# Loads of x from batch 2 on issued from ScalarE's queue, not from SyncE's

## The chip, the cores and the metric

The kernel runs on one core of a Trainium2 chip. The metric is device time in microseconds (us). The core has five engines that run their own instruction streams in order and meet at semaphores: PE (TensorE), DVE (VectorE), ACT (ScalarE), POOL (GpSimd) and SP (SyncE), which only issues DMAs here. DMAs issued from SP form SP's queue ("SPq" in the profile), those issued from ACT form ACT's ("ACTq").

## What is computed

```python
x = L0_attn_t                                   # (16, 1024, 256) float32
x = x + layernorm(attention(layernorm(x)))      # one head, 256 wide, W_qkv (768, 256) and a bias
x = x + layernorm(ffn(layernorm(x)))            # ffn: down(silu(gate(x)) * up(x)), hidden 768
# attention: softmax(Q K^T / 16) V; the ffn weights are integers times 1/127
```

Every float32 operand is split into a high and a low float16 part, and a product is two or three float16 matmul passes (high by high, high by low, low by high).

## The kernel before, in words

The 16 batches of 1024 rows are worked off in a software pipeline: while PE does the scores of batch b+1, it does the attention output of batch b and then its ffn. Each batch is cut into two halves g (512 rows). The order of the work is written out by hand for every engine; there is no scheduler. Batches 0, 14 and 15 have an order of their own, the ones between run through a loop.

The steps that the change and the prediction touch:

- x is loaded from HBM twice. `load_x(b, g)` (L213) loads a half into `xs`, from which the first layernorm (`x_stats` on DVE, `x_norm` on POOL, `x_hat` on ACT) and the split into `xh` and `xl` (`x_high` on ACT, `x_low` on POOL) are made. It waits until `x_low` of the batch before has read `xs`. `reload(b, g)` (L229) loads the same half into one of four buffers `X`, to which the attention's result is added (`x1_add`, DVE, L664). It waits until the store from that buffer, two batches before, has landed.
- `turn_x`, `turn_p`, `turn_y` (L218, L237, L247) are DMA transposes in SBUF, each for a high and a low part: `xTh`/`xTl`, `PTh`/`PTl` (the softmax numerators), `yTh`/`yTl` (the ffn's input). `store` (L254) writes the result out. All of them are issued by SP, in one hand-written order, with a wait ahead of each. In the period of batch b the loads stand behind `turn_x(b+2, 1)` and ahead of `turn_p(b+1, 7)` and `turn_y(b, 1)`.
- The ffn's input of a half is made in this chain: `x1_norm` (POOL, writes `nb`), `y_hat` (ACT, L458, writes `yn`), `y_high` (ACT, L465, writes `yh`), `y_low` (POOL, L365, writes `yl`), `turn_y` (SP, L251), and then `gate_up` on PE, which needs both transposes.
- `exp` (ACT, L438) and `p_high` (ACT, L445) make a block of softmax numerators; `p_low` (L338) is the low part. `silu` (ACT, L473) and `h_high` (ACT, L480) belong to the ffn. Exp and silu need different function tables, so that ACT loads a table at each change between them (ACT_TABLE_LOAD).
- All matmul passes are issued in one helper, L710, so PE's rows carry that line. PE's `gate_up(b, g, c)` waits for its PSUM bank with a `silu_done` count, as in `gate_up(t, 0, 0, 4, 2, (silu_done, 2), (hmul_done, 2), three)` (L1796).

Of the kernel before, what the change touches and what calls it, by code (L numbers as in the profile page):

```python
# [40 lines left out]
def sandwich(nc, x_d, wqkv_d, b_d, wg_d, wu_d, wd_d, out_d):  # L41
# [8 lines left out]
    with ctx:  # L50
# [162 lines left out]
        def load_x(s, b, g):  # L213
            xl_wait(s, b - 1, g)
            s.engine.dma_start(xs[:, 4 * g:4 * g + 4, :],
                               x_d[b, :, :].rearrange("(p t) d -> p t d", t=NT)[:, 4 * g:4 * g + 4, :]).then_inc(xs_in[g], 16)
# [12 lines left out]
        def reload(s, b, g):  # L229
            k = (2 * b + g) % 4  # L230
            s.wait_ge(stored[k], 32 * (b // 2))
            if b < 2:
                s.wait_ge(ffn_turned[b], 32)
            s.engine.dma_start(X[k][:, :, :], x_d[b, :, :].rearrange("(p t) d -> p t d", t=NT)[:, 4 * g:4 * g + 4, :]
                               ).then_inc(X_in[k], 16)
# [608 lines left out]
        def _(engine):  # L844
# [23 lines left out]
            turn_p(s, 0, 3, 1)  # L868
            turn_x(s, 1, 1, 0)
            turn_x(s, 1, 1, 1)  # L870
            load_x(s, 2, 0)
            load_x(s, 2, 1)
            turn_p(s, 0, 4, 0)
            turn_p(s, 0, 4, 1)
            turn_p(s, 0, 5, 0)
# [10 lines left out]
            turn_p(s, 1, 0, 1)  # L886
            turn_ffn(s, 2, 0)
            turn_ffn(s, 2, 1)
            reload(s, 0, 0)
            reload(s, 0, 1)  # L890
            turn_p(s, 1, 1, 0)
            turn_p(s, 1, 1, 1)
            turn_p(s, 1, 2, 0)
# [8 lines left out]
            turn_y(s, 0, 0, 1)  # L902
            turn_x(s, 2, 1, 0)
            turn_x(s, 2, 1, 1)
            load_x(s, 3, 0)
            load_x(s, 3, 1)
            turn_p(s, 1, 5, 0)
            turn_p(s, 1, 5, 1)
            turn_p(s, 1, 6, 0)
# [3 lines left out]
            turn_p(s, 1, 7, 0)  # L913
            turn_p(s, 1, 7, 1)
            for b in range(1, 13):
                reload(s, b, 0)
                reload(s, b, 1)
                turn_p(s, b + 1, 0, 0)
                turn_p(s, b + 1, 0, 1)
                store(s, b - 1, 0, 0)  # L920
                store(s, b - 1, 0, 1)
                turn_p(s, b + 1, 1, 0)
                turn_p(s, b + 1, 1, 1)
                turn_p(s, b + 1, 2, 0)
                turn_p(s, b + 1, 2, 1)
                turn_p(s, b + 1, 3, 0)
                turn_p(s, b + 1, 3, 1)
                turn_p(s, b + 1, 4, 0)
                turn_p(s, b + 1, 4, 1)
                turn_y(s, b, 0, 0)  # L930
                turn_y(s, b, 0, 1)
                turn_x(s, b + 2, 0, 0)
                turn_x(s, b + 2, 0, 1)
                turn_p(s, b + 1, 5, 0)
                turn_p(s, b + 1, 5, 1)
                turn_p(s, b + 1, 6, 0)
                turn_p(s, b + 1, 6, 1)
                turn_x(s, b + 2, 1, 0)
                turn_x(s, b + 2, 1, 1)
                load_x(s, b + 3, 0)  # L940
                load_x(s, b + 3, 1)
                turn_p(s, b + 1, 7, 0)
                turn_p(s, b + 1, 7, 1)
                turn_y(s, b, 1, 0)
                turn_y(s, b, 1, 1)
                store(s, b - 1, 1, 0)
                store(s, b - 1, 1, 1)
            reload(s, 13, 0)
            reload(s, 13, 1)
            turn_p(s, 14, 0, 0)  # L950
            turn_p(s, 14, 0, 1)
            store(s, 12, 0, 0)
# [22 lines left out]
            turn_y(s, 13, 1, 1)  # L975
            store(s, 12, 1, 0)
            store(s, 12, 1, 1)
            reload(s, 14, 0)
            reload(s, 14, 1)
            store(s, 13, 0, 0)  # L980
            turn_p(s, 15, 0, 0)
            turn_p(s, 15, 0, 1)
# [18 lines left out]
            turn_p(s, 15, 7, 0)  # L1001
            turn_p(s, 15, 7, 1)
            store(s, 13, 1, 1)
            reload(s, 15, 0)
            reload(s, 15, 1)
            store(s, 14, 0, 0)
            store(s, 14, 0, 1)
            turn_y(s, 15, 0, 0)
# [167 lines left out]
        def _(engine):  # L1176
# [23 lines left out]
            exp(a, 0, 5, 6)  # L1200
            z_high(a, 1, 0, 2)
            p_high(a, 0, 5)
            exp(a, 0, 6, 0)
            p_high(a, 0, 6)
            ffn_high(a, 0)
# [9 lines left out]
            exp(a, 1, 1, 2)  # L1215
            p_high(a, 1, 1)
            x_hat(a, 2, 0)
            exp(a, 1, 2, 0)
            p_high(a, 1, 2)
            exp(a, 1, 3, 2)  # L1220
# [13 lines left out]
            p_high(a, 1, 6)  # L1234
            exp(a, 1, 7, 2)
            p_high(a, 1, 7)
            silu(a, 0, 0, 0, 6)
            y_hat(a, 0, 1, 0)
            y_hat(a, 0, 1, 1)
# [25 lines left out]
            x_hat(a, 3, 0)  # L1265
            h_high(a, 0, 1, 5)
            x_hat(a, 3, 1)
            exp(a, 2, 0, 0)
            p_high(a, 2, 0)
            o_high(a, 1, 0, 1)  # L1270
# [4 lines left out]
            for b in range(2, 14):  # L1275
                p_high(a, b, 1)
                exp(a, b, 2, 0)
                p_high(a, b, 2)
                exp(a, b, 3, 2)
                p_high(a, b, 3)  # L1280
                o_high(a, b - 1, 1, 1)
                exp(a, b, 4, 0)
                p_high(a, b, 4)
                y_hat(a, b - 1, 0, 0)
                y_hat(a, b - 1, 0, 1)
                y_high(a, b - 1, 0)
                o_high(a, b - 1, 1, 0)
                x_high(a, b + 1, 0)
                exp(a, b, 5, 2)
                p_high(a, b, 5)  # L1290
                x_high(a, b + 1, 1)
                exp(a, b, 6, 0)
                p_high(a, b, 6)
                exp(a, b, 7, 2)
                p_high(a, b, 7)
                silu(a, b - 1, 0, 0, 6)
                z_high(a, b + 1, 0, 0)
                h_high(a, b - 1, 0, 0)
                silu(a, b - 1, 0, 1, 2)
                y_hat(a, b - 1, 1, 0)  # L1300
                y_hat(a, b - 1, 1, 1)
                y_high(a, b - 1, 1)
                h_high(a, b - 1, 0, 1)
                silu(a, b - 1, 0, 2, 6)
                h_high(a, b - 1, 0, 2)
                silu(a, b - 1, 0, 3, 0)
                silu(a, b - 1, 0, 4, 2)
                h_high(a, b - 1, 0, 3)
                z_high(a, b + 1, 1, 6)
                h_high(a, b - 1, 0, 4)  # L1310
                silu(a, b - 1, 0, 5, 0)
                silu(a, b - 1, 1, 0, 2)
                h_high(a, b - 1, 0, 5)
                silu(a, b - 1, 1, 1, 6)
                add_bias(a, b - 2, 1, 0)
                h_high(a, b - 1, 1, 0)
                silu(a, b - 1, 1, 2, 0)
                h_high(a, b - 1, 1, 1)
                silu(a, b - 1, 1, 3, 2)
                add_bias(a, b - 2, 1, 1)  # L1320
                h_high(a, b - 1, 1, 2)
                silu(a, b - 1, 1, 4, 6)
                h_high(a, b - 1, 1, 3)
                silu(a, b - 1, 1, 5, 0)
                h_high(a, b - 1, 1, 4)
                h_high(a, b - 1, 1, 5)
                exp(a, b + 1, 0, 0)
                p_high(a, b + 1, 0)
                o_high(a, b, 0, 1)
                add_bias(a, b - 1, 0, 0)  # L1330
                o_high(a, b, 0, 0)
                x_hat(a, b + 2, 0)
                add_bias(a, b - 1, 0, 1)
                exp(a, b + 1, 1, 2)
                x_hat(a, b + 2, 1)
# [48 lines left out]
            silu(a, 13, 1, 5, 0)  # L1384
            h_high(a, 13, 1, 4)
            h_high(a, 13, 1, 5)
            o_high(a, 14, 0, 1)
            o_high(a, 14, 0, 0)
            add_bias(a, 13, 0, 0)
# [42 lines left out]
            h_high(a, 14, 1, 0)  # L1432
            h_high(a, 14, 1, 1)
            silu(a, 14, 1, 2, 0)
            h_high(a, 14, 1, 2)
            o_high(a, 15, 0, 1)
            add_bias(a, 14, 0, 0)
# [581 lines left out]
```

## Time and profile before

| | |
|---|---|
| median of 3 runs | 1376.56 us (1376.06 to 1376.75) |
| profiled execution, its time | 1376.6 us |
| its span in the trace | 1374.7 us |
| PE busy | 1352.9 us, 98% |
| DVE, ACT, POOL busy | 65%, 64%, 60% |
| granted TensorE clock | 0.999 of full speed |
| DMA, queue of SP | 54.4% of the 16 DMA engines' time |

The span runs from the first to the last instruction of the profiled execution; 1.9 us of its time lie around it. PE is the engine that is nearly always busy, so the reader should look for the few places where it is not, and follow from each to what it waited for. Busy shares of the others matter only where they end such a wait.

### The profile page before, as it was taken

Reading aid. Unit: us, or ns where it says so; the run is one execution under the profiler, and the core shown is the slowest. Engines: PE = TensorE matmul, PEld = TensorE weight load, DVE = VectorE, ACT = ScalarE, POOL = GpSimd, SP = SyncE. Lnnn points to the kernel's source line nnn. Section 1 sums busy time; section 2 is a strip of 40 time slices with the busy share of each in tenths; the row PEclk is TensorE's granted clock in tenths of the full one; section 3 lists DMA queues with packets and bytes.
Section 4 is the critical chain, followed back from the end, with each engine's and each line's share of the span. In section 5 each row is a group of like instructions: output and inputs, shape, how many; then the busy total and the mean of one; then the engine's idle time right before and its main releaser. Section 6 shows DMA issues by size and latency. Waiting matters only on the chain.

```text
span 1374.7 us, 22429 instructions
## 1 busy us (share of the span) xinstructions
PE 1352.9 (98%) x7437; PEld 728.8 (53%) x7437; DVE 897.3 (65%) x2160; ACT 877.5 (64%) x1373; POOL 825.2 (60%) x1002
## 2 busy tenths in 40 slices
PE   8999999999999999999999999999999999999997
PEld 4444555554555555555554555545555555555554
DVE  6786666666757667666766657667566666656555
ACT  4757475766756667575675767567566775756644
POOL 2768375573837658476484756748376583745545
PEclk9999999999999999999999999999999999999999
DMA  7996382654727466382753836447383663716411
GB/s 199 188 185 149 68 163 78 116 130 84 147 85 135 104 112 143 77 163 68 137 132 70 161 77 123 123 95 144 78 151 88 123 133 80 141 55 114 94 40 55
DMA packets 437176, 158.29 MB, mean 115 GB/s; under 512 B 418113, under 2 KB 420417, under 8 KB 437058
## 3 DMA queue, kind: packets, MB, share of 16 engines
q1 hardware_dynamic: 436272, 156.03, 54.4%
q8 instruction: 61, 1.00, 0.3%
q10 hardware_dynamic: 786, 0.79, 0.2%
q14 instruction: 57, 0.47, 0.1%
HBM read 36.70 MB, written 16.78 MB: 39 GB/s over the span
## 4 chain that ended last, share of the span: by engine, by line
PE 91%; DVE 3%; SPq 2%; DMA 2%; issue 1%; POOL 1%; ACT 0%; ACTq 0%; POOLq 0%
PE S L710 90%; DMA yTl<-yl 1%; SPq L245 1%; PE S L729 1%; DVE mxs L613 1%; DVE S L642 0%; SPq L226 0%; DVE st L651 0%; POOL rs L293 0%; SPq L251 0%; DMA xTl<-xl 0%; POOL Pl L338 0%; DVE xl L320 0%; POOL yl L365 0%; DVE X L664 0%
## 5 line engine op out<-in xcount | busy, mean ns | idle before, releaser
L438 ACT ACTIVATE P<-S,nmx,sc 128x1024 f32<-128x1024 f32 x128 | 153.6, 1200 | 283.1 <-DVE nmx L617 283.1
L613 DVE TENSOR_REDUCE mxs<-S 128x1 f32<-128x1024 f32 x128 | 156.1, 1220 | 124.7 <-PE S L710 124.4
L679 DVE SCALAR_TENSOR_TENSOR hf<-S,sc,hf 128x512 f32<-128x512 f32 x192 | 141.9, 746 | 140.6 <-ACT hf L473 134.4
L338 POOL TENSOR_TENSOR Pl<-P,Ph 128x1024 f16<-128x1024 f32 x96 | 205.9, 2145 | 33.9 <-issue 26.4
L710 PE MATMUL S<-xTh,zTh 128*128 128x512 f16 x512 | 194.1, 379 | 4.2 <-ACT P L438 2.2
L710 PE MATMUL S<-PTh,xl 128*128 128x512 f16 x512 | 194.0, 379 | 0.0
L710 PE MATMUL S<-xTl,zTh 128*128 128x512 f16 x512 | 194.0, 379 | 0.0
L710 PE MATMUL S<-xTh,zTl 128*128 128x512 f16 x512 | 194.0, 379 | 0.0
L710 PE MATMUL S<-PTl,xh 128*128 128x512 f16 x512 | 194.0, 379 | 0.0
L710 PE MATMUL S<-PTh,xh 128*128 128x512 f16 x512 | 194.0, 379 | 0.0
L289 POOL TENSOR_SCALAR rs<-mv,sc 128x2 f32<-128x2 f32 (+1 forms) x96 | 35.2, 367 | 231.5 <-DVE mv L655 191.8
L710 PE MATMUL S<-Wh,hTh 128*128 128x256 f16 x768 | 170.4, 273 | 1.9 <-DVE X L703 1.7
L374 POOL TENSOR_TENSOR hTl<-hf,hTh 128x512 f16<-128x512 f32 x128 | 146.2, 1157 | 41.0 <-ACT hTh L480 36.7
L710 PE MATMUL S<-Wh,hTl 128*128 128x256 f16 x768 | 170.4, 273 | 0.0
L473 ACT ACTIVATE hf<-S,sc 128x512 f32<-128x512 f32 x192 | 130.7, 682 | 53.1 <-POOL hTl L374 35.4
L293 POOL TENSOR_TENSOR rs<-rs,mhalf 128x4 f32<-128x4 f32 (+1 forms) x160 | 145.0, 906 | 13.3
L710 PE MATMUL S<-yTh,Gh 128*128 128x512 f16 x384 | 145.6, 379 | 4.0 <-DMA yTl<-yl 3.9
L710 PE MATMUL S<-yTl,Gh 128*128 128x512 f16 x384 | 145.5, 379 | 0.0
L710 PE MATMUL S<-yTh,Uh 128*128 128x512 f16 x384 | 145.5, 379 | 0.0
L710 PE MATMUL S<-yTl,Uh 128*128 128x512 f16 x384 | 145.5, 379 | 0.0
L480 ACT ACTIVATE hTh<-hf 128x512 f16<-128x512 f32 x192 | 119.8, 624 | 33.8 <-DVE hf L679 33.8
L445 ACT ACTIVATE Ph<-P 128x1024 f16<-128x1024 f32 x128 | 135.1, 1055 | 5.6 <-DMA PTl<-Pl 2.0
(115 smaller groups left out, 2476.1 us busy)
## 6 DMA issues: line engine op xcount, KB each, us to landing
xs<-in_L_attn_t SPq DMA_DIRECT2D x32, 512.0 KB, 5.3
X<-in_L_attn_t SPq DMA_DIRECT2D x32, 512.0 KB, 4.4
out_x<-X SPq DMA_DIRECT2D x64, 256.0 KB, 2.9
PTh<-Ph SPq DMA_TRANSPOSE x128, 3.2
PTl<-Pl SPq DMA_TRANSPOSE x128, 3.2
hTh<-in_L_attn_W_qkv ACTq DMA_DIRECT2D x1, 768.0 KB, 7.2
hTl<-in_L_ffn_w_gate SPq DMA_DIRECT2D x1, 768.0 KB, 7.4
hTh<-in_L_ffn_w_up SPq DMA_DIRECT2D x1, 768.0 KB, 9.1
```

Of the source, the lines that this page charges most:

```text
L245: s.engine.dma_start_transpose(dst[:, :, c * 128:(c + 1) * 128], src[:, m % 3, :]).then_inc(p_turned[m % 3], 16)
L289: p.engine.tensor_scalar(rs, var, scalar1=eps, scalar2=mul, op0=ALU.add, **({} if mul is None else {"op1": ALU.mult})).then_inc(g_step, 1)
L293: return p.engine.tensor_tensor(out=rs, in0=rs, in1=mhalf[:, 0:rs.shape[1]], op=ALU.pow)
L338: p.engine.tensor_tensor(out=Pl[:, m % 3, :], in0=P[:, m % 2, :], in1=Ph[:, m % 3, :], op=ALU.subtract).then_inc(pl_vector if i in PL_ON_V ...
L374: p.engine.tensor_tensor(out=hTl[g][:, c, :], in0=hf[:, n % 3, :], in1=hTh[g][:, c, :], op=ALU.subtract).then_inc(hl_vector if c in HL_ON_ ...
L438: a.engine.activation(P[:, m % 2, :], ps[:, bank:bank + 2, :].rearrange("p a n -> p (a n)"), ACT.Exp, bias=nmx[:, c:c + 1], scale=sS, accu ...
L445: a.engine.activation(Ph[:, m % 3, :], P[:, m % 2, :], ACT.Copy).then_inc(ph_done, 1)
L473: a.engine.activation(hf[:, n % 3, :], ps[:, bank, :], ACT.Silu, scale=sc2[:, 3:4]).then_inc(silu_done, 1)
L480: a.engine.activation(hTh[g][:, c, :], hf[:, n % 3, :], ACT.Copy).then_inc(hh_done, 1)
L613: v.engine.tensor_reduce(mxs[:, c:c + 1], ps[:, bank:bank + 2, :].rearrange("p a n -> p (a n)"), axis=AX.X, op=ALU.max, negate=True).then_ ...
L679: v.engine.scalar_tensor_tensor(out=hf[:, n % 3, :], in0=ps[:, bank + 1, :], scalar=sc2[:, 4:5], in1=hf[:, n % 3, :], op0=ALU.mult, op1=AL ...
L710: done = t.engine.matmul(out, s, m, start=(start and i == 0), stop=(stop and i == len(terms) - 1))
```

## The change

The pairs of `load_x` from batch 2 on and all pairs of `reload` leave SP's list and are put into ACT's list, between activations. Functions and waits are unchanged, only the engine that waits and issues differs, and the place in the order. `load_x` of batches 0 and 1, all transposes and all stores stay on SP.

```diff
@@ SP's list
             turn_x(s, 1, 1, 1)
-            load_x(s, 2, 0)
-            load_x(s, 2, 1)
             turn_p(s, 0, 4, 0)
...
-            reload(s, 0, 0)
-            reload(s, 0, 1)
...
-            load_x(s, 3, 0)
-            load_x(s, 3, 1)
...
             for b in range(1, 13):
-                reload(s, b, 0)
-                reload(s, b, 1)
                 turn_p(s, b + 1, 0, 0)
...
                 turn_x(s, b + 2, 1, 1)
-                load_x(s, b + 3, 0)
-                load_x(s, b + 3, 1)
                 turn_p(s, b + 1, 7, 0)
...
-            reload(s, 13, 0), (s, 13, 1), (s, 14, 0), (s, 14, 1), (s, 15, 0), (s, 15, 1)
@@ ACT's list
             p_high(a, 0, 5)
+            load_x(a, 2, 0)
+            load_x(a, 2, 1)
             exp(a, 0, 6, 0)
...
             x_hat(a, 2, 0)
+            reload(a, 0, 0)
+            reload(a, 0, 1)
             exp(a, 1, 2, 0)
...
             p_high(a, 1, 7)
+            load_x(a, 3, 0)
+            load_x(a, 3, 1)
             silu(a, 0, 0, 0, 6)
...
             x_hat(a, 3, 1)
+            reload(a, 1, 0)
+            reload(a, 1, 1)
             exp(a, 2, 0, 0)
...
@@ ACT's loop, for b in range(2, 14)
                 silu(a, b - 1, 0, 1, 2)
+                load_x(a, b + 2, 0)
+                load_x(a, b + 2, 1)
                 y_hat(a, b - 1, 1, 0)
...
                 h_high(a, b - 1, 1, 5)
+                reload(a, b, 0)
+                reload(a, b, 1)
                 exp(a, b + 1, 0, 0)
...
             h_high(a, 13, 1, 5)
+            reload(a, 14, 0)
+            reload(a, 14, 1)
             o_high(a, 14, 0, 1)
...
             silu(a, 14, 1, 2, 0)
+            reload(a, 15, 0)
+            reload(a, 15, 1)
             h_high(a, 14, 1, 2)
```

## Rows read from the trace of the kernel before

**Rows 1.** The page: span and busy time of each engine.

```profile
span 1374.7 us, 22429 instructions
...
PE 1352.9 (98%) x7437; PEld 728.8 (53%) x7437; DVE 897.3 (65%) x2160; ACT 877.5 (64%) x1373; POOL 825.2 (60%) x1002
```

**Rows 2.** Busy time by stretch: stretch, length, busy us of each engine, PE clock, DMA share.

```profile
318.00:401.00 83.00, 83.00 (x457) 44.61 (x456) 54.77 (x132) 54.43 (x87) 51.34 (x62) 1.00 0.54 115
```

**Rows 3.** Waits of PE, whole span: waiter, releaser, total us, times, longest.

```profile
PE S L710 <- DMA yTl<-yl: 3.9, 5, 1.8
```

**Rows 4.** Timeline of PE: start us, us, instruction, [idle before, releaser].

```profile
122.92 0.39 PE L710 MATMUL S<-yTh,Gh 128*128 128x512 f16 x1 [0.20 <-DMA yTl<-yl]
...
705.35 0.39 PE L710 MATMUL S<-yTh,Gh 128*128 128x512 f16 x1 [0.58 <-DMA yTl<-yl]
...
955.11 0.39 PE L710 MATMUL S<-yTh,Gh 128*128 128x512 f16 x1 [0.40 <-DMA yTl<-yl]
...
1267.78 0.39 PE L710 MATMUL S<-yTh,Gh 128*128 128x512 f16 x1 [1.01 <-DMA yTl<-yl]
```

**Rows 5.** Timeline of SP's queue near three of these waits; durations are issue times.

```profile
119.47 1.34 SPq L251 DMA_TRANSPOSE yTl<-yl  x1
...
693.15 1.06 SPq L215 DMA_DIRECT2D xs<-in_L_attn_t  x2
694.25 1.42 SPq L245 DMA_TRANSPOSE PTh<-Ph  x1
695.72 4.98 SPq L245 DMA_TRANSPOSE PTl<-Pl  x1
...
702.10 1.32 SPq L251 DMA_TRANSPOSE yTl<-yl  x1
...
951.87 1.31 SPq L251 DMA_TRANSPOSE yTl<-yl  x1
```

**Rows 6.** Timeline of POOL near the same three waits.

```profile
115.32 2.13 POOL L365 TENSOR_TENSOR yl<-yn,yh 128x1024 f16<-128x1024 f32 x1 [0.71 <-ACT yh L465]
...
689.03 2.12 POOL L320 TENSOR_TENSOR xl<-xs,xh 128x1024 f16<-128x1024 f32 x1
...
698.51 2.13 POOL L365 TENSOR_TENSOR yl<-yn,yh 128x1024 f16<-128x1024 f32 x1 [0.51 <-ACT yh L465]
...
948.62 2.14 POOL L365 TENSOR_TENSOR yl<-yn,yh 128x1024 f16<-128x1024 f32 x1 [0.51 <-ACT yh L465]
```

**Rows 7.** Timeline of ACT at the start: a DMA that ACT issues.

```profile
0.72 0.53 ACTq L395 DMA_DIRECT2D ft<-in_L_attn_b_qkv  x1
```

**Rows 8.** Timeline of ACT at the two places in the loop.

```profile
384.26 0.63 ACT L480 ACTIVATE hTh<-hf 128x512 f16<-128x512 f32 x1 [0.37 <-DVE hf L679]
...
394.61 1.21 ACT L438 ACTIVATE P<-S,nmx,sc 128x1024 f32<-128x1024 f32 x1 [8.41 <-DVE nmx L617]
...
692.19 0.70 ACT L473 ACTIVATE hf<-S,sc 128x512 f32<-128x512 f32 x1
695.27 2.08 ACT L458 ACTIVATE yn<-X,nb,rs 128x256 f32<-128x256 f32 x4 [2.38 <-POOL nb L298]
```

**Rows 9.** A pair of reloads on SP, and reloads on the page (last: us to landing).

```profile
381.60 2.46 SPq L234 DMA_DIRECT2D X<-in_L_attn_t  x2
...
X<-in_L_attn_t SPq DMA_DIRECT2D x32, 512.0 KB, 4.4
```

**Rows 10.** Timeline of DVE: first use of a reloaded X.

```profile
415.24 0.87 DVE L664 SCALAR_TENSOR_TENSOR X<-S,rs,X 128x256 f32<-128x256 f32 x2
```

**Rows 11.** Timeline of ACT and of PE near the loads of batch 3.

```profile
108.13 1.06 ACT L445 ACTIVATE Ph<-P 128x1024 f16<-128x1024 f32 x1
...
115.66 1.25 ACT L473 ACTIVATE hf<-S,sc 128x512 f32<-128x512 f32 x2
...
116.52 0.38 PE L710 MATMUL S<-yTh,Gh 128*128 128x512 f16 x1
```

**Rows 12.** Busy time of a stretch of 1 us while loads land, columns as in rows 2.

```profile
365.00:366.00 1.00, 1.00 (x6) 0.48 (x5) 0.00 (x0) 1.00 (x2) 0.39 (x2) 1.00 0.98 389
```

More of the change, by code:

```diff
@@ L947, in _ @@
                 store(s, b - 1, 1, 1)
-            reload(s, 13, 0)
-            reload(s, 13, 1)
             turn_p(s, 14, 0, 0)
@@ L977, in _ @@
             store(s, 12, 1, 1)
-            reload(s, 14, 0)
-            reload(s, 14, 1)
             store(s, 13, 0, 0)
@@ L1003, in _ @@
             store(s, 13, 1, 1)
-            reload(s, 15, 0)
-            reload(s, 15, 1)
             store(s, 14, 0, 0)
```

## The prediction

> **What bounds the kernel now.** I read the first page, then PE's busy time stretch by stretch, then PE's waits, then each place where PE stood idle, and from there back through SP's queue, POOL and ACT. PE is busy for 98% of the span [rows 1], and the chain is nearly all PE's. From 152 us to 1231 us the kernel repeats a period of 83 us (13 of them), in which PE is busy from end to end; row 2 is one of them [rows 2]. So what another engine or a queue does there shows only where PE is made to wait. The list of PE's waits has one cause that transposes and loads share: the landing of yTl, 3.9 us in five places [rows 3]. Two of these are in the repeated part, 0.58 us at 705.35 and 0.40 us at 955.11; one of 0.20 us is at 122.92, one of 1.01 us at 1267.78 [rows 4]. The fifth, the longest of rows 3 (1.8 us), is at 107 us.
>
> How the two in the repeated part come about: SP issues the two loads of x in 1.06 us, then the transpose to PTh, and then holds for 4.98 us on the transpose to PTl, so that yTl is issued at 702.10 [rows 5]. POOL had yl ready at 698.51 + 2.13 = 700.64 [rows 6]. SP was thus 1.46 us late. At the other place yl was ready at 948.62 + 2.14 = 950.76 and yTl issued at 951.87, 1.11 us late [rows 5, 6]. PE waited 0.58 and 0.40 us, less than SP was late in both. In the other periods SP shows the same hold after the loads, but PE does not wait.
>
> **The change, part by part.**
> Off SP: 28 loads of xs (batches 2 to 15) and 32 reloads of X, in pairs of about 1.06 us. Every transpose on SP behind a pair of loads may start up to 1.06 us sooner. If the long hold of PTl is that SP's own queue is full of the two loads, it goes too; then yTl is issued as soon as yl is there, and the 0.58 and 0.40 us close: **-0.98 us**. The other 10 periods have no PE wait to give back. At 1267.78 no load stands near on SP (the reload of batch 14 is 50 us earlier), so those 1.01 us stay; and at 107 us yTl was issued ahead of the loads of batch 3. The lower bound of this term is nothing (the hold stays), the upper all that rows 3 has, 3.9 us.
>
> Onto ACT, what one pair costs: a DMA that ACT issued in this trace took 0.53 us [rows 7], two of them 1.06, as SP's pair did [rows 5]. I take 1.06. Below that it can be nothing, if ACT's issue runs beside the activation before it; above I use 2.46, SP's pair of reloads with a wait in it [rows 9].
>
> *Loads in the loop, 12 times*, stand between a silu and y_hat. The silu starts at 692.19 and takes 0.70; y_hat starts at 695.27 and stood idle for 2.38 us for POOL's nb [rows 8]. 1.06 fits in 2.38, and even 2.46 leaves only 0.08. The wait that comes along (x_low of the batch before) is on POOL ahead of a p_low and the x1_norm that y_hat waits for: xl ended at 689.03 + 2.12 = 691.15 [rows 6], before the silu began. So the wait is met. Cost 0. Without that cover, 1.06 us a period would go into the chain y_hat, y_high, y_low, yTl, against 704.77 - (700.64 + 0.05 + 3.20) = 0.88 us that yTl could then be late (704.77 is when PE could have begun; 3.20 is what yTl took to land).
>
> *Reloads in the loop* stand ahead of exp(b+1, 0), after the last h_high at 384.26 + 0.63. That exp begins at 394.61 after 8.41 us idle [rows 8], with the table load of 1.28 us ahead of this idle time. Their wait is for the stores of two batches before; SP met the same wait by 381.60 + 2.46 = 384.06 [rows 9], before ACT is there. Cost 0, with over 7 us to spare. X then lands some 4.4 us after issue [rows 9], near 390.5; its first use is at 415.24 [rows 10]. Cost 0. The pairs outside the loop, read off ACT's timeline in the same way, stand in or just ahead of idle time of ACT that is longer than a pair, but for the reload of batch 15, which lacks 0.1 us, and for the next one.
>
> *Loads of batch 3* are the one place without cover: behind p_high(1, 7), with the table load and silu(0, 0, 0) right behind it. ACT is then in arrears up to the silu pair at 115.66, whose first ends near 116.30; gate_up(0, 0, 4) needs it and starts at 116.52 [rows 11]: 0.22 us of slack. A delay d of ACT becomes d - 0.22 on PE. The ends are d = 0 and 1.06 (0 and 0.84 us); activations start before the last one has ended and the issue may lie under the 1.06 us of p_high, so I take the middle, 0.53: **+0.31 us**. The later yTl is not hurt: POOL made yl ready at 115.32 + 2.13 = 117.45 [rows 6], which becomes 117.98, and SP issued yTl only at 119.47 [rows 5], behind the loads and the same hold. There are 1.49 us to use, so the 0.20 us at 122.92 close: **-0.20 us**.
>
> *DMA engines.* The bytes are the same and the loads start within 1 us of before. In the stretch with loads the engines are near full (0.98 busy at 389 GB/s in the microsecond at 365 us, where loads land) [rows 12], so the work is there on any queue; what may change is who stands behind whom.
>
> **Sum:** -0.98 + 0.31 - 0.20 = -0.87 us. The profiled execution took 1376.6 us (span 1374.7), the median of the runs 1376.56, so the sum is applied as it stands: 1375.7.
>
> **Rivals.**
> *The hold stays.* The hold of PTl is the DMA engines at work on the loads, not SP's queue. Then the transposes issued beside the loads share the engines with them, PTl is held as long as before, and yTl gains nothing. For it: rows 12. Against it: yTl comes last and the work ahead of it, two loads and two transposes, must anyway be over before yl is ready. Time: 0 for the two gaps, and 0 to 0.84 us at batch 3: 1376.6 to 1377.4, say 1377.0. The Trainium skill, "DMA: Bandwidth & Descriptors", section "Issuing engines are not separate DMA queues", says that DMAs from different engines run on the same 16 DMA engines and interleave, and that only the sequencer's issue time is saved. By that rule alone this rival holds; its sum would be 1377.0 against my 1375.7. The trace of before can't decide, as all loads in it beside transposes come from SP.
>
> *ACT is held at its issue (the other side).* If ACT's pair of loads meets the hold that PTl met, the in-order engine stops before y_hat. Place: the 12 periods. It decides from 2.38 + 0.88 = 3.26 us per pair; at 3.5 us the loss, 12 x 0.24, passes 0.2%. With a first load of 0.53 and a second held as PTl was, 4.98 us, a pair takes 5.5: 12 x 2.25 = 27 us, and 5.3 at batch 3, so up to 1409. Against it: SP's own two loads, right behind transposes, took 1.06 us and were never held; the one held is the second transpose after them [rows 5], and ACT's queue carries nothing else.
>
> *More than two gaps go.* If transposes land sooner without loads ahead of them, all 3.9 us could close: 1372.7. Against it: at 107 us and 1267.78 no load stands ahead.
>
> **How the numbers follow.** Forecast 0.50 (1375.7, own range 1375.2 to 1376.4); hold stays 0.30 (1377.0); ACT held 0.10 (over 1379.3); more gaps 0.04; the rest, an unforeseen shift of 1 to 2 us at the ends, 0.06. The runs spread by 0.7 us, and about 0.2% (2.75 us) is what can be told from no change. The range runs from 1374.4, with part of the other gaps closed, to 1378.8, which is a pair of 2.46 us on ACT (2.24 at batch 3) and no gap closed. Faster 0.04, same 0.85, slower 0.11.
>
> **What would show it.** PTl after the loads takes about 1.3 us at issue and not 3 to 5; yTl is issued within 0.1 us of yl's end; the waits of PE for yTl are near 2.7 us, not 3.9; ACT's idle time before y_hat is near 1.3 and not 2.4 us; a gap of 0.3 us or so opens in PE near 115 to 117 us; ACT's pair takes about 1.06. The prediction is wrong if ACT's idle time before y_hat is gone and PE waits for yTl in every period.

## The result, and the profile after

The changed kernel takes 1424.84 us (median of 6 runs), the kernel before 1376.53 in the same series: 1.036 times as long, 95% interval 1.034 to 1.038. That is 48 us slower, where 1375.7 was forecast and 1378.8 was the upper end.

The page after, and PE's waits (waiter, releaser, total us, times, longest):

```profile
span 1425.1 us, 22429 instructions
...
PE 1369.6 (96%) x7437; PEld 731.6 (51%) x7437; DVE 897.8 (63%) x2160; ACT 881.4 (62%) x1373; POOL 822.0 (58%) x1002
...
q1 hardware_dynamic: 427632, 124.57, 48.1%
q10 hardware_dynamic: 9426, 32.25, 8.6%
```

```profile
PE S L710 <- DMA xTl<-xl: 35.0, 11, 5.4
PE S L710 <- DMA yTl<-yl: 2.8, 4, 1.0
```

Against [rows 3] the wait for yTl has shrunk from 3.9 to 2.8 us, and a new one is there: PE waits for xTl, the low part of the transposed x of batch b+2, 35.0 us in 11 places. Nine of them are in the loop; of the other two one is at the start, as before (1.4 us against 1.3), and one of 0.91 us at 59.84. The span is 50.4 us longer. PE's idle time grew from 1374.7 - 1352.9 = 21.8 to 1425.1 - 1369.6 = 55.5 us, that is by 33.7. The other 16.7 us are PE's own: the same 7437 matmuls are busy for longer.

One of these places, on SP's queue, on ACT and on PE (start us, us, instruction, [idle before, releaser]):

```profile
193.90 1.34 SPq L226 DMA_TRANSPOSE xTh<-xh  x1
195.28 1.34 SPq L226 DMA_TRANSPOSE xTl<-xl  x1
196.67 3.94 SPq L245 DMA_TRANSPOSE PTh<-Ph  x1
200.66 8.36 SPq L245 DMA_TRANSPOSE PTl<-Pl  x1
209.11 1.33 SPq L251 DMA_TRANSPOSE yTh<-yh  x1
```

```profile
195.14 0.33 ACTq L215 DMA_DIRECT2D xs<-in_L_attn_t  x1
195.20 0.64 ACT L480 ACTIVATE hTh<-hf 128x512 f16<-128x512 f32 x1
195.52 0.48 ACTq L215 DMA_DIRECT2D xs<-in_L_attn_t  x1
195.72 0.69 ACT L473 ACTIVATE hf<-S,sc 128x512 f32<-128x512 f32 x1
198.77 2.08 ACT L458 ACTIVATE yn<-X,nb,rs 128x256 f32<-128x256 f32 x4 [2.36 <-POOL nb L298]
```

```profile
209.41 0.61 PE L710 MATMUL S<-xTh,Ah 128*128 128x512 f16 x1 [5.43 <-DMA xTl<-xl]
209.81 0.63 PE L710 MATMUL S<-xTl,Ah 128*128 128x512 f16 x1
```

The same place on SP's queue in the kernel before:

```profile
193.14 1.35 SPq L226 DMA_TRANSPOSE xTl<-xl  x1
194.53 1.06 SPq L215 DMA_DIRECT2D xs<-in_L_attn_t  x2
195.63 1.68 SPq L245 DMA_TRANSPOSE PTh<-Ph  x1
197.36 3.10 SPq L245 DMA_TRANSPOSE PTl<-Pl  x1
```

The two loads are issued by ACT within 0.4 us, just as SP issues xTl. xTl lands at 209.4, 14.1 us after issue (4.6 before). Of the two loads the first lands 5.5 us after issue and the second, caught in the same stall, 13.7. SP is then held for 3.9 and 8.4 us at the next two transposes, where it took 1.7 and 3.1 before (and 1.4 and 5.0 in the period of [rows 5]). ACT pays nothing: the two DMA instructions run beside activations, and its idle time before y_hat is 2.36 us, as before.

What xTl took to land, whole span, of the kernel before and then of the one after:

```profile
DMA to landing us min/median/max: 3.1/3.3/5.0
```

```profile
DMA to landing us min/median/max: 3.2/4.2/14.1
```

For the second halves in the 12 periods of the loop it is 3.1 to 4.9 us before (the loads are issued 1.4 us behind xTl), and after it is 10.8 to 14.1 in nine and 6.9 to 7.6 in three. PE wanted it 8.7 us after issue here (PE was ready at 203.98) and 7.8 to 8.7 in the 12, so it waits in the nine and not in the three. The nine and the three differ in the moment: in the nine ACT issued the first load 0.1 to 0.4 us ahead of SP's xTl, in the three 0.75 and 0.91 us ahead of it or 0.24 behind it.

The stretch of the wait, in slices of one us (columns as in [rows 2]: the last three are the granted PE clock, the DMA share and GB/s):

```profile
202.00:203.00 1.00, 1.00 (x7) 0.44 (x5) 0.00 (x0) 1.00 (x2) 0.99 (x1) 1.00 1.03 169
...
205.00:206.00 1.00, 0.00 (x0) 0.00 (x0) 1.00 (x2) 0.78 (x2) 1.00 (x2) 1.00 1.72 23
206.00:207.00 1.00, 0.00 (x0) 0.00 (x0) 1.00 (x2) 0.54 (x2) 1.00 (x2) 1.00 0.87 53
207.00:208.00 1.00, 0.00 (x0) 0.00 (x0) 0.90 (x3) 0.12 (x1) 1.00 (x2) 0.67 1.30 71
208.00:209.00 1.00, 0.00 (x0) 0.00 (x0) 0.00 (x0) 0.00 (x0) 0.92 (x2) 0.50 1.23 42
...
213.00:214.00 1.00, 1.00 (x4) 0.30 (x2) 0.72 (x1) 0.00 (x0) 0.00 (x0) 0.50 0.08 16
214.00:215.00 1.00, 1.00 (x6) 0.45 (x5) 0.00 (x0) 0.46 (x1) 0.00 (x0) 0.92 0.00 0
```

Two things are to be seen. The DMA engines count as fully busy while they move 23 to 71 GB/s, where they move 389 in [rows 12] and 210 with transposes alone (share 1.12, at 105 us of the kernel before): they are occupied and hardly move data. (A packet's whole time is counted in the slice in which it starts, so a slice can show a share above 1.) And PE, idle since 203.98, is granted 1.2 GHz instead of 2.4 from 207.3 to 214.1 us: the matmuls after the wait follow each other in 0.43 us instead of 0.22. The clock fell so behind seven of the nine waits in the loop (2.87 to 5.43 us long), not behind the other two (2.19 and 2.82 us), and also near 105 and 1412 us. This is where the 16.7 us of longer PE busy time lie; the mean granted clock fell from 0.999 to 0.987, and 1.2% of 1425 us is 17 us.

### The profile page after: what moved, and what is told of

It reads as the page before. It is cut to its first block, busy times and chain, and to the rows that moved or that the text cites. A ratio compares the mean times of both kernels' runs of the same rounds, so it can differ in the third digit from the quotient of the medians.

```text
span 1425.1 us, 22429 instructions
## 1 busy us (share of the span) xinstructions
PE 1369.6 (96%) x7437; PEld 731.6 (51%) x7437; DVE 897.8 (63%) x2160; ACT 881.4 (62%) x1373; POOL 822.0 (58%) x1002
## 4 chain that ended last, share of the span: by engine, by line
PE 80%; DMA 8%; DVE 4%; SPq 4%; issue 2%; ACT 2%; POOL 1%; ACTq 0%; POOLq 0%
PE S L710 79%; DMA xTl<-xl 7%; SPq L245 2%; SPq L226 1%; DVE mxs L613 1%; DVE S L642 1%; DVE st L651 1%; DMA yTl<-yl 1%; ACT Ph L445 1%; PE S L729 1%; ACT P L438 0%; POOL Pl L338 0%; DVE mv L655 0%; DVE nmx L617 0%; SPq L251 0%
## 5 line engine op out<-in xcount | busy, mean ns | idle before, releaser
L710 PE MATMUL S<-xTh,zTh 128*128 128x512 f16 x512 | 194.7, 380 | 5.1 <-ACT P L438 2.2
L710 PE MATMUL S<-xTh,zTl 128*128 128x512 f16 x512 | 194.7, 380 | 0.0
L710 PE MATMUL S<-xTl,zTh 128*128 128x512 f16 x512 | 194.6, 380 | 0.0
L710 PE MATMUL S<-PTh,xh 128*128 128x512 f16 x512 | 194.1, 379 | 0.1
L710 PE MATMUL S<-PTl,xh 128*128 128x512 f16 x512 | 194.1, 379 | 0.0
L710 PE MATMUL S<-PTh,xl 128*128 128x512 f16 x512 | 194.1, 379 | 0.0
L710 PE MATMUL S<-Wh,hTh 128*128 128x256 f16 x768 | 172.0, 274 | 1.9 <-DVE X L703 1.7
L710 PE MATMUL S<-Wh,hTl 128*128 128x256 f16 x768 | 172.0, 274 | 0.0
L293 POOL TENSOR_TENSOR rs<-rs,mhalf 128x4 f32<-128x4 f32 (+1 forms) x160 | 145.0, 906 | 13.3
L710 PE MATMUL S<-yTh,Gh 128*128 128x512 f16 x384 | 145.8, 380 | 3.8 <-DMA yTl<-yl 2.8
L710 PE MATMUL S<-yTh,Uh 128*128 128x512 f16 x384 | 145.6, 379 | 0.0
L710 PE MATMUL S<-yTl,Gh 128*128 128x512 f16 x384 | 145.6, 379 | 0.0
L710 PE MATMUL S<-yTl,Uh 128*128 128x512 f16 x384 | 145.6, 379 | 0.0
```

What stands on the lines that cost most here:

```text
L293: return p.engine.tensor_tensor(out=rs, in0=rs, in1=mhalf[:, 0:rs.shape[1]], op=ALU.pow)
L710: done = t.engine.matmul(out, s, m, start=(start and i == 0), stop=(stop and i == len(terms) - 1))
```

## The experiments

Times are medians with the ratio to the kernel before run on the same chip. All kernels but the bare stages compute the whole reference. The theories that the texts below name A to G are each stated where they first come up. "The place of the changed kernel" is between silu(b-1, 0, 1) and y_hat(b-1, 1, 0) on ACT. The loads of batches 2 and 3, ahead of the loop, go to ACT in e2_load_only and e10_merged alone, and the reloads in e1_reload_only and e10_merged alone; elsewhere they stay on SP.

### Which of the moved loads it is

**e1_reload_only**: only the reloads move.

```diff
 SP:   (all load_x as before; every reload removed)
 ACT:  reload(a, b, 0); reload(a, b, 1)      # at the places of the changed kernel; no load_x
```

> Only the reloads of X are issued from ACT; the loads of xs stay on SP as before. Theory A (copies from ACT's queue slow the transposes of SP's queue while both are in flight): in the loop the reloads stand where SP issues no transposes, so the time is that of before, 1376.5 us within 1.5 us. Theory B (the loads of xs start ahead of the transposes of x, on whatever queue): also 1376.5. Theory C (any traffic on ACT's queue costs, wherever it stands): a good part of the 48 us, 1395 or more.

Measured: 1376.19 us, ratio 1.000 (0.999 to 1.001). The reloads cost nothing, as forecast, so ACT's queue in itself is not the cause: theory C falls.

**e2_load_only**: only the loads of xs from batch 2 on move.

```diff
 SP:   (every reload as before; load_x from batch 2 on removed)
 ACT:  load_x(a, b + 2, 0); load_x(a, b + 2, 1)      # and batches 2 and 3; no reload
```

> Only the loads of xs are issued from ACT, at the places of the changed kernel; the reloads of X stay on SP. Theory A (copies of ACT's queue beside transposes of SP's queue): all of the loss is here, 1420 to 1430 us, with PE waiting some 35 us for xTl. Theory C (any traffic on ACT's queue): clearly less than the whole loss.

Measured: 1429.32 us, ratio 1.038 (1.034 to 1.042). PE's wait for xTl is 39.5 us in 12 places. The loss lies wholly in the loads of xs.

### Queue, order or moment

**e3_sp_early**: the order of the changed kernel, on one queue.

```diff
+                load_x(s, b + 3, 0)
+                load_x(s, b + 3, 1)
                 turn_x(s, b + 2, 1, 0)
                 turn_x(s, b + 2, 1, 1)
-                load_x(s, b + 3, 0)
-                load_x(s, b + 3, 1)
```

> All loads on SP, but in the loop the pair of loads of xs is moved ahead of the pair of transposes to xTh and xTl, so that it starts as early as in the changed kernel. Theory A (two queues): xTl lands 3 to 7 us after issue and PE waits for it little or not at all, 1376 to 1382 us. Theory B (order alone): xTl lands 10 us or more after issue, PE waits for it in most periods, 1400 us or more.

Measured: 1376.56 us, ratio 1.000 (0.999 to 1.001).

```profile
191.00 1.14 SPq L215 DMA_DIRECT2D xs<-in_L_attn_t  x2
192.19 1.25 SPq L226 DMA_TRANSPOSE xTh<-xh  x1
193.48 3.60 SPq L226 DMA_TRANSPOSE xTl<-xl  x1
```

With 1 MB queued ahead of it, xTl lands in 4.8 to 7.7 us in the loop, and PE waits for it 0.1 us at most. Bytes and order explain 1 to 4 us of landing, not 11. Theory B falls. (SP's pairs are issued 0.6 to 0.8 us apart here and ACT's 0.4 in the changed kernel; the bare stages below bear on that.)

**e4_act_quiet** and **e5_sp_quiet**: the pair is issued where no transposes are in flight, from ACT and from SP.

```diff
 e4, ACT:                h_high(a, b - 1, 1, 2)
+                load_x(a, b + 2, 0)
+                load_x(a, b + 2, 1)
 e5, SP:                 turn_y(s, b, 1, 1)
+                load_x(s, b + 3, 0)
+                load_x(s, b + 3, 1)
                 store(s, b - 1, 1, 0)
```

> In the loop the loads of xs are issued from ACT, but some 15 us later, behind the third h_high of the second half, where SP has no transposes in flight; all else as before. Theory A: no transposes beside them, and no hold of PTl behind them either, so 1375.0 to 1376.5 us. Theory C (ACT's queue costs anywhere): well over 1390 us.

> The same later place with SP as the issuer: in the loop the pair of loads of xs stands behind the transposes to yTh and yTl of the second half. Every theory: PTl is held no longer, yTl is issued as soon as yl is there, the two waits of PE of 0.58 and 0.40 us close: 1375.0 to 1376.5 us. With the run before it, it tells whether the queue matters at all when no transposes are near.

Measured: 1375.08 us, ratio 0.9992 (0.9982 to 1.0001), and 1374.75 us, 0.9992 (0.9983 to 1.0002). Away from transposes the queue makes no difference. Both intervals still include no change. In both, PE's wait for yTl is 2.9 us in 2 places: the gaps of 0.58 and 0.40 us of [rows 4] are gone, and that of 0.20 us too, although the loads of batch 3 stand where they stood. SP's queue in e5_sp_quiet, at the period that had the longest hold in [rows 5]:

```profile
691.97 1.33 SPq L245 DMA_TRANSPOSE PTh<-Ph  x1
693.34 1.49 SPq L245 DMA_TRANSPOSE PTl<-Pl  x1
697.28 1.23 SPq L251 DMA_TRANSPOSE yTh<-yh  x1
699.49 1.24 SPq L251 DMA_TRANSPOSE yTl<-yl  x1
700.77 1.06 SPq L215 DMA_DIRECT2D xs<-in_L_attn_t  x2
```

The hold of PTl (4.98 us) is gone, and yTl is issued 0.03 us after yl is ready (697.33 + 2.13 on POOL).

**e6_one_load**: one of the two loads at the place of the changed kernel, the other on SP as before.

```diff
 SP:                     load_x(s, b + 3, 0)
-                load_x(s, b + 3, 1)
 ACT:                    silu(a, b - 1, 0, 1, 2)
+                load_x(a, b + 2, 1)
                 y_hat(a, b - 1, 1, 0)
```

> In the loop one of the two loads of xs (the second half) is issued from ACT at the place of the changed kernel, the other stays on SP behind the transposes to xT; reloads on SP. Theory A in its plain form (the slowing lasts as long as ACT's queue has copies in flight, here half the bytes): xTl lands 7 to 9 us after issue, PE waits little, 1378 to 1395 us. If one copy is enough to upset the transposes whatever its size: 1410 us or more.

Measured: 1375.15 us, ratio 0.9995 (0.9986 to 1.0005). xTl lands in 5.0 to 6.7 us. Half the bytes from ACT's queue at this place cost nothing at all, less than either reading expected.

**e7_after_xT**: the pair waits until xTh and xTl have landed.

```diff
                 silu(a, b - 1, 0, 1, 2)
+                a.wait_ge(x_turned[1], 32 * (b + 2))
+                load_x(a, b + 2, 0)
+                load_x(a, b + 2, 1)
                 y_hat(a, b - 1, 1, 0)
```

> In the loop the pair of loads of xs is issued from ACT at the place of the changed kernel, but behind a wait until the transposes to xTh and xTl ahead of it have landed; only those to PTh, PTl, yTh and yTl are still in flight beside it. Theory A: xTl lands after 3 to 4 us and PE waits for it no more; the slowing falls on PTl and on yTl, which lands late, so that PE waits there: 1385 to 1415 us. If only the transposes ahead of the loads are slowed: about 1376 to 1380 us, with ACT's short wait.

Measured: 1387.1 us, ratio 1.008 (1.007 to 1.010). The time fell into theory A's range, but not for its reason. xTl lands in 3.3 to 5.0 us in the loop. PE's waits there (152 to 1240 us) show that yTl's grew, from 1.0 to 2.1 us, and that the largest new one is another:

```profile
PE S L710 <- ACT hf L473: 5.8, 7, 1.7
PE S L710 <- DMA yTl<-yl: 2.1, 4, 1.0
```

ACT, which stands and waits for the transposes, is late with what PE needs next. PTl, in flight when the loads are issued, lands in 6.5 to 8.2 us in nine of the 12 periods and in 3.2 to 4.1 in the other three. That is twice and more what it takes in e4_act_quiet (3.1 to 4.5), but little more than in the kernel before (5.7 to 7.2) and far from the 11 to 14 of xTl. yTh and yTl, issued some 4 us and more after the loads, land in 3.0 to 5.8 and 3.0 to 4.4, and SP is held at no transpose of the loop for more than 2.4 us. So the pair of loads does slow what it meets here too, but with PTl and the end of PTh in flight and no transpose right behind them the stall does not come. Whether the number of transposes or the moment matters, this run doesn't tell.

**e8_apart**: both loads on ACT, the second 5.8 us after the first.

```diff
                 silu(a, b - 1, 0, 1, 2)
+                load_x(a, b + 2, 0)
                 y_hat(a, b - 1, 1, 0)
                 y_hat(a, b - 1, 1, 1)
                 y_high(a, b - 1, 1)
+                load_x(a, b + 2, 1)
```

> In the loop both loads of xs are issued from ACT, the first at the place of the changed kernel, the second some 5 us later, behind y_high; all else as before. The plain form of theory A has fallen (in the bare stages two loads from ACT cost no more than two from SP, and with one load from ACT the kernel lost nothing). Theory D (two copies queued on ACT at once beside a full queue of transposes is what upsets them): xTl lands in 5 to 7 us, 1375 to 1378 us. Theory E (bytes from ACT's queue within the stretch of transposes, however spaced): 1400 us or more.

Measured: 1375.25 us, ratio 1.000 (0.999 to 1.001). xTl lands in 4.6 to 7.0 us. The same 1 MB from ACT's queue, over the same run of transposes, costs nothing once the two DMAs are apart.

**e10_merged**: the changed kernel, with each pair made one DMA of 1 MB.

```diff
+        def load_both(s, b):
+            xl_wait(s, b - 1, 0)
+            xl_wait(s, b - 1, 1)
+            s.engine.dma_start(xs[:, :, :], x_d[b, :, :].rearrange("(p t) d -> p t d", t=NT)).then_inc(xs_in[0], 16)
...
-                load_x(a, b + 2, 0)
-                load_x(a, b + 2, 1)
+                load_both(a, b + 2)
```

> The changed kernel, with each pair of loads of xs from ACT (512 KB each) made one load of 1 MB, at the same places; the reloads from ACT as they are. Theory F (two copies in ACT's queue, close together, beside a queue full of transposes): xTl lands in 5 to 8 us, PE waits for it little, 1375 to 1380 us. Theory G (1 MB from a second queue beside the transposes, however cut; the bare stages are no fair picture of the kernel): 1415 us or more.

Measured: 1385.49 us, ratio 1.0056 (1.0039 to 1.0074). The loss against the kernel before is 9.1 us and not 48.3. PE's waits (L715 is the L710 of the others):

```profile
PE S L715 <- DMA xTl<-xl: 7.2, 4, 2.5
PE S L715 <- DMA yTl<-yl: 2.7, 3, 1.1
```

In the loop xTl lands in 6.2 to 8.5 us in ten periods and in 11.2 and 10.3 in two, the only two where PE waits for it (2.5 and 1.6 us; 1.6 more are at 60.88, ahead of the loop). So most of the loss goes when one DMA takes the place of two; the edit also doubles the packet, from 4 to 8 KB, and makes DVE wait for both halves of x at once. A smaller part stays (the range of theory F is missed by 5 us). Of the 10.0 us that the span is longer than before, 6.2 are idle time of PE (its waits for xTl grew by 5.9) and 3.8 are PE's own, at a mean granted clock of 0.997.

### The disputed cost by itself

Four kernels with nothing but DMAs in stages (their output is not the reference's). A stage begins with a short memset on DVE, which waits for all DMAs of the one before; its length is the distance between two memsets. Each kernel ran once, and each kind of stage comes three or four times in it. **m1_beside**: six transposes of 256 KB, copies from the start (the edit in outline).

```diff
+for n, st in enumerate(stages):                 # SP
+    s.wait_ge(go, n + 1)
+    for i in range(6):
+        if (st == "sp_first" and i == 0) or (st == "sp_third" and i == 2): two loads
+        turn(s, i)
+# ACT, after the same wait: two loads, two loads in 1 KB rows, two stores, or one load
```

> The disputed cost by itself; nothing of the reference is computed (the output is zeros). 32 stages, each with six transposes of 256 KB (SBUF to SBUF) from SP and nothing else but: no copy; two loads of 512 KB from SP ahead of them; the same behind the second transpose; two loads from ACT at the same time; the same with rows of 1 KB and not 4 KB; two stores of 512 KB from ACT; two loads from GpSimd; one load from ACT. Each four times. Theory A: a stage takes some 10 us alone, 12 to 13 with the loads on SP at either place, and 18 us or more with the two loads from ACT; GpSimd as ACT. Theory B (order and bytes): all stages with two loads from 12 to 14 us, whatever the queue. The stages with 1 KB rows, with stores and with one load tell whether the size of a packet, the direction or the bytes set it.

The memsets of the first stages (none, SP first, SP third, ACT), from the timeline of DVE:

```profile
6.29 0.07 DVE L69 MEMSET mark<- 128x8 f32 x1
16.50 0.07 DVE L69 MEMSET mark<- 128x8 f32 x1 [10.14 <-DMA tr<-src]
29.63 0.07 DVE L69 MEMSET mark<- 128x8 f32 x1 [13.07 <-DMA tr<-src]
43.13 0.07 DVE L69 MEMSET mark<- 128x8 f32 x1 [13.44 <-DMA tr<-src]
56.22 0.07 DVE L69 MEMSET mark<- 128x8 f32 x1 [13.02 <-DMA tr<-src]
```

| stage | us, four times (the last kind three times) |
|---|---|
| none | 10.1 to 10.2 |
| two loads, SP, ahead / behind the second | 13.1 / 13.3 to 13.5 |
| two loads, ACT | 13.0 to 13.3 |
| two loads, ACT, 1 KB rows / two stores | 12.3 / 12.6 to 12.7 |
| two loads, GpSimd | 13.9 to 15.1 |
| one load, ACT | 11.6 |

Two loads from ACT cost what two from SP cost. Theory A as I had stated it fell here, with e6_one_load.

**m2_phase**: eight transposes, loads from ACT started later and later.

```diff
+for _ in range(k):                              # ACT, k short activations, each waited for
+    a.activation(junk, junk, ACT.Copy).then_inc(step, 1)
+    done += 1
+    a.wait_ge(step, done)
+load(a, n, 0)
+load(a, n, 1)
```

> The disputed cost by itself again, now with eight transposes in the kernel's pattern (two to PTh and PTl, two to xTh and xTl, then the same again), and the loads from ACT started later and later into them: after 0 to 11 short activations of some 0.6 us; two loads, or one; and for comparison none, and two from SP behind the fourth transpose. Nothing of the reference is computed. Theory D1 (a matter of the moment at which the loads meet the running transposes): some start times give stages longer by 5 us or more than that with the loads on SP. If all start times give about the same stage, what upsets the transposes is something else that only the kernel has, its other engines at work.

| stage | us, three times (one load, k = 4: twice) |
|---|---|
| none | 12.8 to 13.1 |
| two loads, SP, behind the fourth transpose | 16.1 to 16.4 |
| two loads, ACT, k = 0, 1 | 15.4 to 15.9 |
| k = 2 | 18.8 to 19.9 |
| k = 3 | 17.3 to 17.9 |
| k = 4 | 18.8 to 21.4 |
| k = 5 | 17.3 to 18.3 |
| k = 6 | 19.0 to 20.4 |
| k = 7, 9, 11 | 16.2 to 18.4 |
| one load, ACT, k = 2, 4 | 14.2 to 14.9 |

The slowing is there without PE at work: two loads that meet running transposes cost 1 to 5 us more than the same from SP (theory D1 had 5 us or more, which one stage reached); at the very start, as in m1_beside, nothing. The landings show the moment, as in the kernel. At k = 2, 4 and 6 ACT issued the first load within 0.1 us of one of SP's transposes, and that transpose landed in 10.4 to 13.0 us; at k = 3 and 5 it issued it 0.7 us away from the nearest, and the slowest landed in 8.2 to 9.3. The slow stage k = 4 (102.2 to 123.6 us) is the kernel's stall over again, on the queues and in the slices of one us: xT lands in 13.0 us and the second load in 12.7, SP is held, and the DMA engines are busy at a low rate:

```profile
104.97 0.83 ACTq L48 DMA_DIRECT2D LA<-in_L_attn_t  x2
104.97 4.85 SPq L75 DMA_TRANSPOSE xT<-src  x2
109.87 7.72 SPq L75 DMA_TRANSPOSE PT<-src  x1
```

```profile
111.00:112.00 1.00, 0.00 (x0) 0.00 (x0) 0.00 (x0) 1.00 0.95 174
...
114.00:115.00 1.00, 0.00 (x0) 0.00 (x0) 0.00 (x0) 1.00 1.31 72
...
116.00:117.00 1.00, 0.00 (x0) 0.00 (x0) 0.00 (x0) 1.00 2.00 51
...
118.00:119.00 1.00, 0.00 (x0) 0.00 (x0) 0.00 (x0) 1.00 1.28 286
```

**m3_kinds**: other copies at k = 2, 4 and 6.

```diff
+KINDS = ["two", "merged", "halves", "one", "rows", "stores", "pool"]
+# two loads of 512 KB; one of 1 MB; two of 256 KB; one of 512 KB; two in 1 KB rows; two stores; two from GpSimd
```

> Bare stages of eight transposes again (nothing of the reference is computed), with different copies from ACT started after 2, 4 and 6 short activations, the moments that cost most: two loads of 512 KB; one load of 1 MB; two loads of 256 KB; one of 512 KB; two of 512 KB in rows of 1 KB; two stores of 512 KB; two loads from GpSimd. If the count of copies in ACT's queue sets it, the one of 1 MB is as cheap as bytes want (16 us) and two of 256 KB are dear (18 us or more). If bytes set it, the one of 1 MB is as dear as the pair (19 us) and the two of 256 KB are cheap (14.5 us). If the size of a packet sets it, the pair in rows of 1 KB is cheap (16 us) and all with 4 KB dear.

| copies | k = 2 | k = 4 | k = 6 |
|---|---|---|---|
| two of 512 KB | 16.4 to 17.5 | 16.6 to 18.5 | 18.7 to 19.5 |
| one of 1 MB | 15.9 | 15.9 to 16.1 | 16.0 to 16.1 |
| two of 256 KB | 15.9 to 16.2 | 15.9 to 16.7 | 16.1 to 16.8 |
| one of 512 KB | 14.3 to 14.7 | 14.0 to 14.6 | 14.1 to 14.4 |
| two of 512 KB, 1 KB rows | 15.3 to 16.9 | 15.9 to 17.0 | 16.8 to 16.9 |
| two stores of 512 KB | 15.8 to 16.0 | 16.5 to 17.0 | 15.6 to 15.8 |
| two of 512 KB, GpSimd | 16.4 to 16.9 | 16.9 to 18.0 | 18.1 to 19.3 |

One of 1 MB costs no more than two of 512 KB from SP (16.1 to 16.4 in m2_phase), in every case. Two of 256 KB cost 1.4 to 2.3 us more than one of 512 KB in the median, the same bytes. So at equal bytes two DMAs cost more than one, though less than the 18 us and more that the count alone was expected to give. The packets differ as well (8 KB in the one of 1 MB, 4 KB in the pair, 2 KB in the two of 256 KB), but packets of 1 KB are in the median no dearer than those of 4 KB, and at k = 6 cheaper by 1.9 us, so the larger packet is hardly what makes the one DMA cheap. Stores are slowed less than loads. GpSimd's queue behaves as ACT's.

**m4_gap**: activations between the two loads (0, 1, 3, 6), and a second load of 64 KB.

```diff
 load(a, n, 0)
+for _ in range(gap):
+    a.activation(junk, junk, ACT.Copy).then_inc(step, 1)
+    done += 1
+    a.wait_ge(step, done)
 load(a, n, 1)
```

> Bare stages of eight transposes (nothing of the reference is computed), copies from ACT after 4 and 6 short activations: two loads of 512 KB with 0, 1, 3 and 6 activations of some 0.6 us between them; one load of 512 KB with a second of 64 KB right behind it; one of 1 MB. Theory F: 18 to 19 us with no gap at 6, falling to 16 us as the gap grows. If the second load's bytes matter, the small second one costs nothing (14.5 us); if its being there does, 16 us or more.

| | k = 4 | k = 6 |
|---|---|---|
| no gap | 19.4 to 20.4 | 18.9 to 22.1 |
| 1 activation | 15.1 to 15.9 | 15.1 to 17.0 |
| 3 | 16.0 to 17.9 | 15.0 to 18.3 |
| 6 | 15.8 to 16.3 | 15.7 to 16.0 |
| second load of 64 KB | 14.4 to 14.6 | 14.4 to 14.7 |
| one of 1 MB | 15.7 to 16.1 | 15.8 to 16.2 |

A gap of one short activation, which sets the two loads some 1.0 us apart instead of 0.4, takes off 4.6 and 5.2 us in the median, with packets and bytes unchanged. This is the cleanest evidence that it is the closeness of two large DMAs. More is not better: with three activations (2.4 us apart) five of the eight stages took 17.4 us and more. A small second load costs nothing, so it is not their number alone. Nor is it the spacing alone: SP's pairs are 0.6 us apart in m2_phase and harmless, while one pair from ACT in m3_kinds (k = 6) was 0.66 us apart and took 18.7.

### The loads moved in time, all on SP

**e9_sp_quiet_all**: e5_sp_quiet, and the loads of batch 3 also behind the transposes.

```diff
             turn_x(s, 2, 1, 1)
-            load_x(s, 3, 0)
-            load_x(s, 3, 1)
...
             turn_p(s, 1, 7, 1)
+            load_x(s, 3, 0)
+            load_x(s, 3, 1)
```

> All on SP as in the kernel before; the loads of xs in the loop stand behind the transposes to yTh and yTl, and those of batch 3 behind the last transposes of batch 1, so that no loads of xs stand ahead of a transpose from batch 3 on. Every theory now held: the waits of PE of 0.20, 0.58 and 0.40 us close, 1375.0 to 1375.8 us.

Measured: 1374.67 us against 1376.74, ratio 0.9986 (0.9976 to 0.9995). A gain of 0.1%, with an interval that excludes no change; the forecast of it was 1375.0 to 1375.8. In the profiled runs PE's idle time is only 0.6 us less than before, so most of it is not shown to come from the waits. PE's wait for yTl is 3.0 us in 2 places. The two left are the ones at 107 and 1267 us, ahead of which no load stands.

## Why the prediction was wrong, point by point

- **What bounds the kernel**: right. PE is the bound, and the whole loss came through waits of PE.
- **The step that failed** is the paragraph on the DMA engines: "the bytes are the same and the loads start within 1 us of before ... so the work is there on any queue; what may change is who stands behind whom". From this the prediction took no price: it put the transposes' landing at no change, without a run that showed it. It went on to follow yTl alone, the transpose behind the loads, and never asked for xTl, the one ahead of them. On SP's queue the loads were issued 1.4 us behind xTl; on ACT's queue nothing keeps them behind it. PE takes xTl up 7.8 to 8.6 us after its issue in the trace of before, a margin that could have been read there, and it landed in 10.8 to 14.1 in nine periods.
- Sharing alone would have been harmless here: with one load, with two loads apart or on SP ahead of xTl, it lands in under 8 us. What no row of before shows, and the bare stages do, is that two large loads, issued some 0.4 us apart from a second queue just as SP issues one of several transposes, slow all of them far beyond their bytes. The prediction had said that the trace could not decide between its rivals, as all loads beside transposes came from SP, and yet gave a range of 4.4 us.
- **Second term left out**: PE's clock. Of the 50 us, 33.7 are idle time and 16.7 are matmuls at the lower level, mostly after a wait of several us. On average each us of idle time cost about 1.5.
- **-0.98 us for the two gaps**: half right. The loads cause the hold, and without them beside the transposes it goes: e4_act_quiet, e5_sp_quiet and e9_sp_quiet_all show no gap there, by moving the loads in time. But loads in SP's own queue are not all of it. In the changed kernel none is there, and PTh and PTl are held for 12.3 us together and not 1.3 each; in e8_apart, where the stall does not come, PTh is still held for 2.1 to 2.8 us in the loop, against 1.2 to 1.3 in e4_act_quiet. The sign that PE's waits for yTl would be near 2.7 us came out (2.8) by luck: they lie at 108, 303, 562 and 1316 us, and in the loop two new ones took the place of the two old.
- **-0.20 us at 122.92**: no such wait is left, but e4_act_quiet and e5_sp_quiet lack it as well, with the loads of batch 3 on SP. So the move is not shown to have closed it.
- **ACT's cost in the loop, 0**: right, and smaller than argued. The pair takes 0.33 + 0.48 us and lies under activations; the idle time before y_hat is 2.36 us, as before, where 1.3 had been forecast.
- **Reloads, 0**: right (e1_reload_only).
- **Loads of batch 3, +0.31**: wrong, though a gap came at the forecast place. It is 1.00 us at 117.19, where 0.3 had been forecast at 115 to 117 us, and PE waits there for `zw`, which DVE makes behind ACT's `z_high`, and not for silu. The loads did not make it. ACT was already late at the exp ahead of them, for which these are the rows of before and of after:

```profile
106.80 1.20 ACT L438 ACTIVATE P<-S,nmx,sc 128x1024 f32<-128x1024 f32 x1 [0.20 <-DVE nmx L617]
```

```profile
109.36 1.20 ACT L438 ACTIVATE P<-S,nmx,sc 128x1024 f32<-128x1024 f32 x1 [1.56 <-DVE nmx L617]
```

  DVE was late with nmx because PE was late with the scores: its granted clock stood at 0.50 there (105 to 108 us), and at 1.00 in the kernel before. From the start of p_high to the table load, with the pair of loads between them, ACT took 1.14 us, and 1.07 before: the pair cost 0.07 us, not 0.53. e2_load_only has the same loads at the same place, the clock at 1.00 and no gap. Why the clock fell there in one run and not in the other, after the same wait of 2.19 us, is not shown.
- **"The hold stays"** was right that the hold of PTl would not go with the loads off SP's queue, but its price, 0.4 us, was not. **"ACT is held"** was wrong: ACT was not held (a pair of loads takes 0.8 to 1.2 us). It was the only rival far on the slower side, with 0.10, and for the wrong mechanism.
- The Trainium skill, "DMA: Bandwidth & Descriptors", section "Issuing engines are not separate DMA queues", says that spreading DMAs over engines saves only issue time. As advice this case bears it out: nothing was won. As a price it falls short: the same DMAs cost 48 us more on two queues than on one. The Trainium skill, same page, section "Queues, rings and completion order", says that an engine takes turns between queues, a packet from each. The 5 to 7 us that xTl takes with one load of the pair on ACT's queue agrees with such sharing; the 14.1 us with both does not follow from it.

**What stays open**: why two loads close together do it and one of the same bytes hardly. The DMA engines are recorded as busy at 23 to 71 GB/s, so something in them waits, but no view here shows for what. Nor is it shown why some tenths of a microsecond between the load's issue and the transpose's decide, why a gap of three activations is dearer than one of one, or why the same pair cost 19 us in one kernel of bare stages and 17 in another at k = 2.

## What to carry to other kernels

Moving a DMA to another engine's queue removes an order: ask which transfers stood ahead of it on the old queue, when they are needed, and whether they still land in time. Here transposes from SP with several microseconds of margin were safe beside one load of 512 KB from another queue, but not beside two issued together; set two such loads apart (by 1 us or by 5.8 it was harmless here, by 2.4 not always), merge them, which took away most of the loss, or leave them on the queue of the transposes. If transposes are held behind loads, the loads are better moved in time, to where no transposes are in flight, than to another queue. And where PE is near 100% busy, waits of 3 to 5 us cost more than their length: here about one and a half times, as PE's clock is lower for a while behind most of them.

## What the hardware showed that was not expected

- A transpose of 256 KB that lands in 3.1 to 4.9 us took up to 14.1 with two 512 KB loads from a second queue beside it, and the second of the loads up to 13.7; eight transposes and the pair took 18.9 to 22.1 us with no gap between the loads and 15.1 to 17.0 with one activation of some 0.6 us between them.
- One load of 1 MB in place of the pair: 15.7 to 16.2 us.
- After PE stood idle from 203.98, its granted clock was at 1.2 GHz from 207.3 to 214.1 us and matmuls came every 0.43 us; PE had resumed at 209.41.
- ACT issues a DMA while its own activation runs: 0.33 and 0.48 us at 195.14 and 195.52, beside the activations around them, and its idle time before y_hat was not changed.
- Some tenths of a microsecond decide: with the first load issued 0.1 to 0.4 us ahead of xTl the transpose took 10.8 us and more, with 0.75 or 0.91 us ahead or 0.24 behind 7.6 and less.
